# Denominators' columns moved onto the values' product, and two groups of products reordered, in a delta-rule attention kernel with an expert layer

## The chip, the cores and the metric

The kernel runs on one core of a Trainium2 chip. The metric is the device time of one execution in microseconds, as the median of several runs. One more execution was recorded by the hardware profiler; all rows below come from it. The engines are TensorE (PE, with its weight loads as PEld), VectorE (DVE), ScalarE (ACT), GpSimd (POOL) and SyncE (SP), which here only issues DMAs.

## The reference

Two sequences of 2048 rows of 128 numbers go through a linear attention layer with the delta rule, a layer norm, a layer of eight experts with top-2 routing and a capacity of 640 slots per expert and batch entry, and another layer norm.

```python
q, k = (x @ Wq), (x @ Wk)                 # 4 heads of 128
v, g = (x @ Wv), (x @ Wg)                 # 4 heads of 32
beta = sigmoid(x @ Wb)                    # one number per row and head
k = k * rsqrt(sum(k * k) + 1e-12);  q = q * 128 ** -0.5
# per row t:  delta = (v_t - k_t^T S) * beta_t;  S = S + k_t delta^T;  o_t = q_t^T S
o = o * rsqrt(mean(o * o) + 1e-5) * norm_w * silu(g)
x = layernorm(x + o @ Wo)
x = layernorm(x + moe(x))                 # top 2 of 8 experts, capacity, silu(h1) * h3 @ w2
```

## The kernel before, in words

**Tiling.** The recurrence is worked in 16 chunks of 128 rows, both sequences side by side. Within a chunk and head the deltas come from a triangular system of 128x128, whose inverse is built in levels: 16x16 blocks are inverted by elementwise steps on GpSimd (the first chunk on VectorE), and TensorE joins them to blocks of 32 (`z_32`, `w_32`), 64 (`z_64`, `w_64`) and 128 (`z_128`, `w_128`), each level being two groups of small products on tiles of 32x32 or 64x64 of the array. The right-hand side needs beta, which enters as the denominator 1 + exp(-x Wb) on the diagonal.

**Steps.** All engines run one loop of steps, `for p in range(NP + LAST)`, written out by hand: step p of TensorE does `keys` of chunk p, `values` of chunk p-1, the queries and the 32 and 64 levels of chunk p-4, the 128 level, deltas, new state and outputs of chunk p-5, and the projection of p-6. The order of the `at(...)` lines is the order on the engine. An engine waits in this order; nothing overtakes.

**Products in two forms.** `products` (lines 648 to 655) multiplies a weight matrix by the two sequences' 256 columns. For chunks 0 to 4 it is one float32 product. From chunk 5 (`XF`) on, both operands are split into a high and a low part of type float32r, and three one-pass products take its place. The split weights lie in tiles that the experts use later, so they are named `w13h` and `w13l` in the rows, and the split inputs `xeTh` and `xeTl`. `hb` is where the key-key products go.

**`values`** (line 669) makes, for each sequence, a float32 product with the inputs as the weights and the 128 columns of Wv streaming (line 672), which leaves rows on the partitions. Then `products` with the 4 columns of Wb as the weights makes the logits of beta, 4 partitions by 256 columns. ScalarE's `values_out` (line 1011) takes the exponential into `eb` and copies the values.

**The denominators' way.** SyncE stores `eb` to DRAM (`send_blocks`, line 520) and loads it back as 64 partitions by 16 (`load_blocks`, line 532), the form in which the 16x16 blocks are scaled; the blocks of the key-key product go the same way (`ab`), and so does their diagonal (`ssd`), which ScalarE's `key_norms` reads. SyncE does not send the blocks of a chunk before the loads of the chunk before have landed.

**Banks.** All products that ScalarE or VectorE carry off go through three PSUM banks in turn. A group in `STEP_FILLS` waits until the group three places before it has been carried off: `values` waits for the first of the two copies of `keys`, `key_key` for the second (and needs both for its operand).

**ScalarE's order** around the change is: norms of the heads (`head_norms`, line 1095, which waits for TensorE's `head_sums`), the two key copies, the copies of the diagonal blocks of 32, `values_out`, the high part of the inputs, and then at the head of the next step the copy of `z_128` and that of `key_key`.

The lines of TensorE's products by name:

| name | line | tile of the array |
|---|---|---|
| `products`, float32 / one-pass | 650 / 653 to 655 | full |
| `values` | 672 | full |
| `key_key`, `key_query` | 679, 694 | full |
| `z_32`, `w_32`, `z_64`, `w_64` | 708, 718, 728, 738 | 32x32 |
| `z_128`, `w_128` | 750, 762 | 64x64 |
| `state_keys` | 776 | 128x32 |
| `turn_keys`, `project` | 783, 852 | full |
| `head_sums` | 837 | full |

## Time and profile before

| what | value |
|---|---|
| median of 3 runs | 535.98 us (535.22 to 536.87) |
| the profiled execution | 539.49 us, span of its instructions 537.7 us |
| mean granted clock of TensorE | 0.961 |
| busy time TensorE | 490.4 us (91%), weight loads 408.4 us (76%) |
| busy time VectorE, ScalarE, GpSimd | 330.7, 332.4, 319.7 us (61%, 62%, 59%) |
| chain that ended last, by engine | TensorE 71%, DMA 9%, GpSimd 7% |
| DMA queue of SyncE and its like (q1) | 114864 packets, 29.60 MB, 27.0% of 16 engines |

The span divides into a start with round trips through DRAM (to about 82 us), steady attention steps (to about 254 us), the last attention steps, in which no new chunk begins, and from about 330 us on the experts and the last layer norm. The time of a product in a timeline includes its way through the array, so products that follow each other overlap there. The chain of waits counts each only from the end of the one before.

### The profile page before, as it was taken

What the parts mean: (1) busy time and instruction counts of PE and PEld (TensorE: products, weight loads), DVE (VectorE), ACT (ScalarE), POOL (GpSimd) and SP (SyncE); (2) the same over time, 40 slices, a digit from 0 to 9 for tenths busy, and PEclk for the clock granted to TensorE, in tenths of its full rate; (3) what the DMA queues carried; (4) which work ended last, traced back from release to release, by engine and by line L of the source; (5) the groups of instructions that cost most, each with busy time, mean ns of one, the idle gap of its engine ahead of it and who ended that gap; (6) DMA issues with size and microseconds to landing.
All of it is one profiled execution on the core that took longest, in us unless ns stands there. A gap on an engine that the chain in (4) does not pass through costs nothing.

```text
span 537.7 us, 18954 instructions
## 1 busy us (share of the span) xinstructions
PE 490.4 (91%) x7096; PEld 408.4 (76%) x7096; DVE 330.7 (61%) x1316; ACT 332.4 (62%) x916; POOL 319.7 (59%) x441
## 2 busy tenths in 40 slices
PE   6989999999999999999979977999999999999900
PEld 4666767767777777776656667999999999999900
DVE  4436567767687676876955872565455654555344
ACT  3646777777777877777743642554555545555456
POOL 3053528757578575785883452376677766767650
PEclk9999999999999999999985998999999999999975
DMA  3358753762545725436383234254555545553366
GB/s 93 31 86 226 257 112 44 107 93 31 66 46 59 102 33 72 49 46 99 34 166 39 27 33 109 36 109 55 108 107 76 109 55 108 93 85 36 31 135 204
DMA packets 136820, 45.83 MB, mean 85 GB/s; under 512 B 89568, under 2 KB 131296, under 8 KB 136736
## 3 DMA queue, kind: packets, MB, share of 16 engines
q1 hardware_dynamic: 114864, 29.60, 27.0%
q0 software_dynamic: 20288, 9.51, 19.4%
q10 hardware_dynamic: 1584, 5.59, 2.6%
q8 instruction: 54, 0.88, 0.7%
q14 instruction: 30, 0.25, 0.1%
HBM read 21.13 MB, written 23.55 MB: 83 GB/s over the span
## 4 chain that ended last, share of the span: by engine, by line
PE 71%; DMA 9%; POOL 7%; issue 5%; SPq 3%; ACT 2%; DVE 1%; POOLq 1%; ACTq 0%; DVEq 0%
PE ps L956 19%; PE ps L970 13%; PE ps L694 4%; PE ps L679 4%; POOL slots_in L1665 3%; PE ps L650 3%; PE ps L653 3%; PE ps L654 2%; PE ps L655 2%; POOL xs L1648 2%; PE ps L914 2%; PE ps L718 2%; POOL prod L1647 2%; DMA a_diag<-hb 1%; PE ps L728 1%
## 5 line engine op out<-in xcount | busy, mean ns | idle before, releaser
L1706 POOL DMA_INDIRECT x_store<-xk,row x80 | 123.9, 1549 | 68.5 <-ACT xk L1214 45.8
L1665 POOL DMA_INDIRECT slots_in<-x,slot x64 | 98.7, 1542 | 25.6 <-issue 17.3
L1540 DVE TENSOR_TENSOR hb<-ps,hs 128x320 f32<-128x320 f32 (+1 forms) x128 | 62.7, 491 | 53.1 <-ACT hs L1206 52.6
L1206 ACT ACTIVATE hs<-ps 128x320 f32<-128x320 f32 (+1 forms) x128 | 55.7, 435 | 34.5 <-PE ps L956 33.5
L970 PE MATMUL ps<-w2s,hb 128*128 128x128 f32 x640 | 74.1, 275 | 0.0
L970 PEld LDWEIGHTS ps<-w2s,hb 128*128 128x128 f32 x640 | 72.8, 192 | 0.0
L956 PE MATMUL ps<-xeTh,w13h 128*128 128x320 f32 x224 | 71.3, 318 | 0.9 <-DVE xeTl L1564 0.9
L956 PE MATMUL ps<-xeTl,w13h 128*128 128x320 f32 x224 | 69.9, 312 | 0.0
L956 PE MATMUL ps<-xeTh,w13l 128*128 128x320 f32 x224 | 69.9, 312 | 0.0
L1214 ACT ACTIVATE xk<-ps,gs 128x128 f32<-128x128 f32 x80 | 24.1, 364 | 45.4 <-PE ps L970 45.4
L1647 POOL TENSOR_TENSOR prod<-a,xs 128x28 f32<-128x28 f32 (+11 forms) x120 | 32.5, 271 | 25.5 <-DVE xs L1375 16.7
L956 PEld LDWEIGHTS ps<-xeTh,w13h 128*128 128x128 f32 x224 | 42.8, 191 | 1.1 <-issue 1.1
L1679 POOL TENSOR_TENSOR Vk<-V,sq 128x256 f32<-128x256 f32 x16 | 10.0, 627 | 56.4 <-ACT sq L1046 56.4
L956 PEld LDWEIGHTS ps<-xeTl,w13h 128*128 128x128 f32 x224 | 42.8, 191 | 0.0
L956 PEld LDWEIGHTS ps<-xeTh,w13l 128*128 128x128 f32 x224 | 42.8, 191 | 0.0
L1648 POOL TENSOR_TENSOR xs<-xs,prod 128x28 f32<-128x28 f32 (+11 forms) x120 | 33.9, 283 | 9.4
L1063 ACT ACTIVATE TT<-x32T 32x256 f32<-32x256 f32 x64 | 26.5, 414 | 18.0 <-DVE x L1318 17.5
L653 PE MATMUL ps<-xeTh,w13h 128*128 128x256 f32 (+1 forms) x110 | 36.2, 329 | 0.0
L694 PE MATMUL ps<-gq,xTs 128*128 128x512 f32 x64 | 34.5, 623 | 0.3 <-issue 0.3
L679 PE MATMUL ps<-y,xTs 128*128 128x512 f32 x64 | 34.0, 620 | 0.5 <-ACT eg L1034 0.5
L654 PE MATMUL ps<-xeTl,w13h 128*128 128x256 f32 (+1 forms) x110 | 31.0, 282 | 0.0
L655 PE MATMUL ps<-xeTh,w13l 128*128 128x256 f32 (+1 forms) x110 | 30.8, 280 | 0.0
(210 smaller groups left out, 1085.3 us busy)
## 6 DMA issues: line engine op xcount, KB each, us to landing
slots_in<-zeros ACTq DMA_DIRECT2D x10, 520.0 KB, 5.0
xe<-slots_in SPq DMA_DIRECT2D x15, 325.0 KB, 2.9
w<-w_in SPq DMA_DIRECT2D x8, 448.0 KB, 4.0
xTs<-xT SPq DMA_DIRECT2D x4, 512.0 KB, 5.1
a_diag<-hb SPq DMA_DIRECT2D x64, 32.0 KB, 1.9
inv<-xs SPq DMA_DIRECT2D x16, 128.0 KB, 2.7
xi<-inv SPq DMA_DIRECT2D x16, 128.0 KB
xk<-x SPq DMA_DIRECT2D x8, 256.0 KB, 4.0
```

Of the source, the lines that this page charges most:

```text
L653: mm(to, hi, xhs[:, r], start=True, stop=False)
L654: mm(to, hi, xls[:, r], start=False, stop=False)
L679: mm(ps[:, to, :], xTs[:, b, cols(n)], y[:, n % YR, b].rearrange("p h t -> p (h t)"), start=True, stop=True).then_inc(fill_mm, 1)
L694: mm(ps[:, to, :], xTs[:, b, cols(n)], gq[:, n % 2, b].rearrange("p h t -> p (h t)"), start=True, stop=True).then_inc(fill_mm, 1)
L956: last = mm(ps[:, HB[fill % 5], 0:HALF], w_[:, P * c:P * c + P], x_[:, par, cols], start=(t == 0), stop=(t == 2))
L970: last = mm(result_at(i), hb[:, par, c, P * i:P * i + P], w2s[:, we, c, :], start=(c == 0), stop=(c == FC))
L1206: af(hs[to, s % 4, :], ps[src, HB[fill_of(s) % 5], 0:HALF], ACT.Silu).then_inc(hs_ready, 1)
L1540: v.tensor_tensor(hb[rows_, par, c, HALF * g:HALF * g + HALF], ps[rows_, at, 0:HALF], hs[rows_, s % 4, :], ALU.mult).then_inc(h_ready, 1)
L1647: link(g.tensor_tensor(pr_, bc(a16[r, j + 1:, j], 2, j + 1), bc(xs[r, 0, j, 0:j + 1], 1, m), ALU.mult))
L1648: link(g.tensor_tensor(xs[r, 0, j + 1:, 0:j + 1], xs[r, 0, j + 1:, 0:j + 1], pr_, ALU.subtract))
L1665: g.indirect_dma_start(out=xs_d[:, :], out_offset=bass.IndirectOffsetOnAxis(ap=to, axis=0), in_=x1[:, p % 2, j, k, :], in_offset=None, com ...
L1706: g.indirect_dma_start(out=x1_d[:, :], in_=ye[:, par, i, :], in_offset=None, out_offset=bass.IndirectOffsetOnAxis(ap=row[:, par, i:i + 1], ...
```

## The change

The four columns of Wb stream behind the 128 columns of Wv, so that one product per sequence gives 132 columns. The exponentials then lie as 128 partitions by 2x4. They are stored to DRAM row by row (128 rows of 8 numbers) and loaded back one number at a time, and the semaphore for that load becomes two, one for even and one for odd chunks. The split of Wb into high and low parts goes. On TensorE `key_key` of the first sequence moves ahead of `z_128`, and `state_keys` ahead of `head_sums`; on ScalarE the copy of `key_key` moves ahead of that of `z_128`.

```diff
-    bd_d = nc.dram_tensor("den_store", (2, U, P), F32, kind="Internal").ap()
+    bd_d = nc.dram_tensor("den_store", (2, P, U), F32, kind="Internal").ap()
...
-        eb = sb("eb", [H, 2, 2 * P])
+        eb = sb("eb", [P, 2, B, H])
...
-                wait(sp, den_ld, 16 * (n - 1))
-                sp.dma_start(bd_d[n % 2].rearrange("(b h) t -> h b t", b=B),
-                             eb[:, n % 2].rearrange("h (b t) -> h b t", b=B)).then_inc(den_st, 16)
+                wait(sp, den_ld[n % 2], 16 * (n // 2))
+                sp.dma_start(bd_d[n % 2], eb[:, n % 2].rearrange("p b h -> p (b h)")).then_inc(den_st, 16)
...
-                sp.dma_start(denb[half], bd_d[n % 2].rearrange("u (k r) -> (u k) r", r=16)).then_inc(den_ld, 16)
+                sp.dma_start(denb[half].unsqueeze(2), bd_d[n % 2].rearrange("(k r) u -> u k r", r=16).unsqueeze(3),
+                             allow_slow_non_contiguous=True).then_inc(den_ld[n % 2], 16)
...
                 for b in range(B):
-                    mm(ps[:, to, P * b:P * b + P], xTs[:, b, cols(n)], wvb[:, 0:H * DV], start=True, stop=True)
-                products(ps[0:H, to, 256:512].rearrange("p (b t) -> p b t", b=B), wvb[:, H * DV:VW], wbs,
-                         n).then_inc(fill_mm, 1)
+                    last = mm(ps[:, to, VW * b:VW * b + VW], xTs[:, b, cols(n)], wvb[:], start=True, stop=True)
+                last.then_inc(fill_mm, 1)
...
                 at(turn_keys, p - 5)
+                at(key_key, p - 1, 0)
                 at(z_128, p - 5)
-                at(key_key, p - 1, 0)
...
+                at(state_keys, p - 4)
                 at(head_sums, p - 5)
-                at(state_keys, p - 4)
...
-                af(eb[:, n % 2], ps[0:H, src, 256:512], ACT.Exp, scale=-1.0).then_inc(den_out, 1)
+                both = ps[:, src, 0:B * VW].rearrange("p (b c) -> p b c", b=B)
+                af(eb[:, n % 2], both[:, :, H * DV:VW], ACT.Exp, scale=-1.0).then_inc(den_out, 1)
                 wait(act, vk_out, n - VR + 1)
-                af(V[:, n % VR], ps[:, src, 0:256].rearrange("p (b c) -> p b c", b=B), ACT.Copy).then_inc(v_out, 1)
+                af(V[:, n % VR], both[:, :, 0:H * DV], ACT.Copy).then_inc(v_out, 1)
...
+                at(key_key_out, p - 3, 0)
                 at(z128_copy, p - 7)
-                at(key_key_out, p - 3, 0)
...
-                dve.wait_ge(den_ld, 16 * n + 16)
+                for m in chunks_in(q):
+                    dve.wait_ge(den_ld[m % 2], 16 * (m // 2) + 16)
```

**TensorE, the middle of step 6,** from `z_64` to the keys' first product. Before:

```order
L728 MATMUL ps<-x32T,hb 32x32 x16
L837 MATMUL ps<-osq,heads 128x256
L776 MATMUL ps<-y,Zs 32x128 x8
L653 MATMUL ps<-xeTh,w13h 128x256
L654 MATMUL ps<-xeTl,w13h 128x256
```

After, where every line number is one or two lower:

```order
L726 MATMUL ps<-x32T,hb 32x32 x16
L774 MATMUL ps<-y,Zs 32x128 x8
L835 MATMUL ps<-osq,heads 128x256
L652 MATMUL ps<-xeTh,w13h 128x256
L653 MATMUL ps<-xeTl,w13h 128x256
```

`state_keys` (776, now 774) now stands directly behind `z_64`, one small-tile group behind another, so that `head_sums` (837, now 835) is followed by full products.

**TensorE, from `w_64` over the start of step 7 to `w_128`.** Before:

```order
L738 MATMUL ps<-z64,x32 32x32 x16
L672 MATMUL ps<-wvb,xTs 128x128 x2
L653 MATMUL ps<-xeTh,w13h 4x256
L654 MATMUL ps<-xeTl,w13h 4x256
L655 MATMUL ps<-xeTh,w13l 4x256
L783 MATMUL ps<-ident,KSt 128x128 x2
L750 MATMUL ps<-TT,hb 64x64 x8
L679 MATMUL ps<-y,xTs 128x512
L852 MATMUL ps<-wox,og 128x136 x2
L694 MATMUL ps<-gq,xTs 128x512
L762 MATMUL ps<-z128,x64 64x64 x8
```

After:

```order
L736 MATMUL ps<-z64,x32 32x32 x16
L671 MATMUL ps<-wvb,xTs 128x132 x2
L781 MATMUL ps<-ident,KSt 128x128 x2
L677 MATMUL ps<-y,xTs 128x512
L748 MATMUL ps<-TT,hb 64x64 x8
L850 MATMUL ps<-wox,og 128x136 x2
L692 MATMUL ps<-gq,xTs 128x512
L760 MATMUL ps<-z128,x64 64x64 x8
```

The three products with 4 columns of weights are gone, and `key_key` (679, now 677) and `z_128` (750, now 748) have changed places.

**ScalarE, the end of a step and the start of the next,** from the copies of the 32 blocks to those behind `w_128`. Before:

```order
L1072 ACTIVATE x64<-x32 32x4x32 x4
L1014 ACTIVATE eb<-ps 4x256
L1016 ACTIVATE V<-ps 128x256
L1135 ACTIVATE xeTh<-xTs 128x256
L1079 ACTIVATE z128<-ps 128x256
L1021 ACTIVATE hb<-ps 128x512
L1084 ACTIVATE TT<-ps 64x4x64 x2
```

After:

```order
L1071 ACTIVATE x64<-x32 32x4x32 x4
L1013 ACTIVATE eb<-ps 128x8
L1015 ACTIVATE V<-ps 128x256
L1134 ACTIVATE xeTh<-xTs 128x256
L1020 ACTIVATE hb<-ps 128x512
L1078 ACTIVATE z128<-ps 128x256
L1083 ACTIVATE TT<-ps 64x4x64 x2
```

The exponential has 8 columns for 256 on 128 partitions for 4, and the copy of `z_128` (1079, now 1078) stands behind that of `key_key`.

## Rows read from the trace of the kernel before

**Rows 1.** Windows: microseconds, then each engine's busy time, clock, DMA.

```profile
82.00:254.00 172.00, 171.52 (x3478) 125.92 (x3475) 126.95 (x554) 131.10 (x379) 120.92 (x216) 1.00 0.50 65
...
276.00:330.00 54.00, 44.74 (x764) 34.47 (x764) 33.19 (x150) 23.30 (x73) 26.86 (x21) 0.84 0.40 69
```

**Rows 2.** Chain of waits before 82 us: start, duration, what.

```profile
11.29 0.53 PE ps L650 x2
...
33.79 5.30 DMA xTs<-xT
...
45.65 0.52 PE ps L650 x2
...
64.42 5.38 DMA inv<-xs
...
73.13 0.14 issue
...
73.27 0.72 PE ps L708 x52
```

**Rows 3.** Chain of waits in a step: what each TensorE group takes.

```profile
78.78 0.63 PE ps L837 x2
...
79.41 0.57 PE ps L776 x16
...
79.98 0.32 PE ps L653
...
81.51 0.64 PE ps L672 x4
...
82.16 0.12 PE ps L653
```

**Rows 4.** Timeline of ScalarE: start, duration, line, what, count, idle before.

```profile
166.33 0.47 ACT L1098 ACTIVATE oln<-ps,eps 128x256 f32<-128x256 f32 x1 [0.24 <-PE ps L837]
...
167.16 1.25 ACT L1008 ACTIVATE y<-ps 128x512 f32<-128x512 f32 x2
...
169.58 0.37 ACT L1014 ACTIVATE eb<-ps 4x256 f32<-4x256 f32 x1
...
170.57 0.36 ACT L1079 ACTIVATE z<-ps 128x256 f32<-128x256 f32 x1
...
173.26 0.77 ACT L1084 ACTIVATE TT<-ps 64x256 f32<-64x256 f32 x2 [1.35 <-PE ps L762]
```

**Rows 5.** Timeline of TensorE, two steps' `values` among it.

```profile
151.10 0.71 PE L672 MATMUL ps<-wvb,xTs 128*128 128x128 f32 x4
...
165.60 0.70 PE L837 MATMUL ps<-osq,heads 128*128 128x256 f32 x2
...
168.33 0.71 PE L672 MATMUL ps<-wvb,xTs 128*128 128x128 f32 x4
...
172.53 0.68 PE L762 MATMUL ps<-z,x 64*64 64x64 f32 x16
```

**Rows 6.** Issues of two loads by tile: nanoseconds min/median/max, first and last start.

```profile
L537 SPq DMA_DIRECT2D denb<-den_store x16: 464/492/1421, 16.2 to 250.1; - x16
...
L541 SPq DMA_DIRECT2D ssd<-a_diag x16: 660/670/1845, 18.1 to 251.9; - x16
```

**Rows 7.** Windows around the first blocks' and diagonal's loads.

```profile
19.00:20.00 1.00, 1.00 (x4) 0.52 (x3) 0.00 (x0) 0.58 (x2) 0.00 (x0) 1.00 0.95 62
20.00:21.00 1.00, 1.00 (x5) 0.69 (x4) 0.61 (x3) 0.74 (x2) 0.00 (x0) 1.00 0.29 6
```

**Rows 8.** Waits, whole trace: VectorE for the denominators' load.

```profile
DVE denp L1365 <- DMA denb<-den_store: 2.2, 1, 2.2
```

**Rows 9.** Timeline of GpSimd, late in the attention part.

```profile
249.10 0.61 POOL L1679 TENSOR_TENSOR Vk<-V,sq 128x256 f32<-128x256 f32 x1 [4.35 <-ACT sq L1046]
```

**Rows 10.** Timeline of VectorE and TensorE at the entry of the inverse.

```profile
175.89 0.28 DVE L1302 TENSOR_SCALAR xh<-xi,high 128x128 f32<-128x128 f32 x1
...
177.44 0.73 PE L708 MATMUL ps<-xh,hb 32*32 32x16 f32 x64
```

More of the change, by code:

```diff
@@ L312, in build @@
         wgs = [w_[:, 2 * H * D:2 * H * D + H * DV] for w_ in wide]
-        wbs = [w_[:, 2 * H * D + H * DV:2 * H * D + H * DV + H] for w_ in wide]
         xhs, xls = (x_[:].rearrange("p a c -> p (a c)").rearrange("p (r b t) -> p r b t", r=XR, b=B)
@@ L367, in build @@
         den_st = sem("den_st")
-        den_ld = sem("den_ld")
+        den_ld = [sem("den_ld0"), sem("den_ld1")]
         a_st = sem("a_st")
@@ L1138, in weights_high @@
                 af(Mks[0], Mk[:], ACT.Copy)
-                af(wbs[0], wvb[:, H * DV:VW], ACT.Copy)
                 af(wgs[0], wg[:], ACT.Copy)
@@ L1489, in weights_low @@
                 dve.wait_ge(split_act, 1)
-                for parts, whole in ((Mks, Mk[:]), (wbs, wvb[:, H * DV:VW]), (wgs, wg[:]), (Nqs, Nq[:])):
+                for parts, whole in ((Mks, Mk[:]), (wgs, wg[:]), (Nqs, Nq[:])):
                     last = v.tensor_tensor(parts[1], whole, parts[0].bitcast(F32), ALU.subtract)
```

## The prediction

> **What bounds the kernel now.** I read the stretches by engine first, then the chain of waits, then single steps of the timeline. The stretches [rows 1] divide the attention part: from 82 to 254 us TensorE is busy for 171.52 of 172.00 us at a granted clock of 1.00, so every piece of TensorE work that goes away there can shorten the time. After 276 us the clock falls to 0.84 and TensorE waits often, and what bounds the stretch between is in the last point of the steady step. The expert part behind it contains nothing that the change touches.
>
> The chain of waits says what the time before 82 us hangs on [rows 2]. The first product of denominators lies on it (0.53 us at 11.29), then a series of round trips through DRAM in SyncE's queue (the last of them the input load of 5.30 us at 33.79, for which TensorE waits), then TensorE again with another such product (0.52 us at 45.65), then again DMAs (the load at 64.42 takes 5.38 us) until `z_32` starts at 73.27. From there the chain runs on TensorE alone.
>
> In a steady step I read the chain by ends, since the durations of the timeline overlap. It gives what each group really takes from the step [rows 3]. A full product after a group on small tiles is dearer than one after another full product: the keys' first takes 0.32 us after `state_keys`, where a one-pass product of 256 columns behind a full one takes 0.12. So a return from small tiles to full ones costs 0.20 us. `head_sums` (0.63) holds one such return, and `values` (0.64) another.
>
> **The change part by part, for one steady step.**
> 1. Three one-pass products of 4 columns go: 3 x 0.12 = 0.36 us [rows 3]. The values' two products get 132 columns for 128: 0.64 less the return of 0.20 is 0.44 us of streaming, and 4/128 of that is 0.014. Saving 0.35 us. This holds for chunks 5 to 15, which are 11 steps. Chunks 0 to 4 lose a two-instruction product of 0.52 us each instead [rows 2].
> 2. `state_keys` ahead of `head_sums`: the order 32x32, full, 128x32, full becomes 32x32, 128x32, full, full. `head_sums` keeps its return (0.63), the keys' first product behind it falls from 0.32 to 0.12. Saving 0.20 us, in the ten steps that have `head_sums` and keys after 73.27 us. `state_keys` itself is taken at its 0.57 us from either side; a spread of 0 to 0.2 is left for it.
> 3. `key_key` ahead of `z_128`: one return to full tiles is moved from `key_key` to `project`, none goes. Nothing is gained by streaming. `z_128` has its operands earlier than it needs them in either order.
>
> The sum of these would be 0.55 us per step. But edit 2 makes `head_sums` end later, and ScalarE's queue stands behind it: its logarithm, the exponential, then both copies of the keys. The next `values` needs the bank that the first of these copies empties (three fills back), and `key_key`, now second, needs both copies. In the timeline [rows 4, 5] `head_sums` ends at 166.30 (165.60 + 0.70), so `z_64` before it ended at 165.67 (less 0.63). ScalarE's logarithm starts at 166.33, and the first copy of the pair, which starts at 167.16 and takes half of the 1.25, ends at 167.78; `values` starts at 168.33, 0.55 us later. After the change `head_sums` ends at 165.67 + 0.57 + 0.63 = 166.87, 0.57 later, so that copy ends at 168.35. TensorE, by the sums above, would reach `values` at 168.33 - 0.20 = 168.13. It waits 0.22 us and then the way of the semaphore (up to 0.14 us, the gap in front of `z_32` at 73.27 [rows 2]); I take 0.27 in all. Waiting does not hide the return: I take `values` at its full 0.64 + 0.01 behind it. So of the 0.20 of edit 2 nothing is left and 0.07 is lost: 0.35 - 0.07 = 0.28 us per step. The second copy then ends at 168.98 (0.57 after today's 168.41) and `key_key` would start at about 169.2: no wait.
>
> Next in ScalarE's queue: today the copy of `z_128` starts at 170.57 and `w_128` at 172.53 [rows 4, 5], 1.6 us after that copy ended. Now that copy stands behind the one of `key_key` (0.50 more), and behind a queue that is 0.56 later, less about 0.1 for the exponential on 128x8 where 4x256 took 0.37. It ends near 172.0, and `w_128` would start at 172.2. The cover shrinks from 1.6 to about 0.2 us; if it is gone, each 0.1 missing costs 1 us over ten steps.
>
> VectorE runs on from the end of `w_64`, and only follows. The other loop, through GpSimd's solver and the DMA that brings the inverse back, has its result (`xh`) at 176.17 while `z_32` starts at 177.44 [rows 10]: 1.1 us of cover behind the semaphore, of which a faster TensorE eats 0.3 to 0.4. Behind 249.10 us GpSimd sets the pace, but its `Vk` there waited 4.35 us for ScalarE [rows 9], which follows TensorE: that point moves forward by all that the steps before it gained, and the rest keeps its length.
>
> Steady part: 10 steps (chunks 6 to 15, behind 73.27 us) x 0.28 = 2.8 us. From both sides: 0.20 per step if the wait costs 0.15 instead of 0.07 (2.0 us), and 0.55 if there is no wait (5.5 us). I take 2.8, since the copy's end and the reach of TensorE are each read from rows.
>
> **The DMA side.** The store of denominators becomes 128 pieces of 32 bytes for 8 of 512, the load back 1024 pieces of 4 bytes for 64 of 64. The nearest row for that load is the diagonal's, also 1024 elements of 4 bytes: SyncE issues it in 0.67 us (median) where the present load takes 0.49 [rows 6]. The blocks' and the diagonal's loads together, 2048 pieces, hold the 16 DMA engines at 0.95 of the microsecond from 19 to 20 and 0.29 of the next [rows 7], so 1024 pieces are 0.6 us of all engines. In a steady step both are covered: VectorE reads the load a step later, and in the whole trace it waited for it once, for 2.2 us, in the first chunk [rows 8], where it then waits for the blocks anyway. Before 73 us they are not always. The load's issue stands on the path once, ahead of the input load at 33.79 (+0.2), and its 0.6 us stand in a busy queue ahead of that load and ahead of the one at 64.42: 0 to 0.6 each, I take 0.3 each. Against that stand the two products that lie on the chain there, 0.53 and 0.52, less 0.01 each: 1.0 us. Net of the start: 1.0 - 0.2 - 0.6 = 0.2 us gained (bounds: 1.0 gained; 0.4 lost with both collisions whole).
>
> The Trainium skill, "DMA: Bandwidth & Descriptors", Rules for kernel authors, says that a non-contiguous last dimension lowers to one descriptor per element and advises against it. The diagonal's row agrees on the price of issuing (0.67 against 0.49 us). By that rule the load is worse for every chunk; by the rows it matters twice. If it counted in all 16 chunks at 0.6 + 0.2 us, it would take 12.8 us and the kernel would be slower; the single wait in rows 8 speaks against that. Its weaker form is rival D.
>
> **Sum.** 2.8 + 0.2 = 3.0 us. The profiled execution took 539.49 us (span 537.7) and would take 536.5; the median of the runs is 535.98, which gives 533.0.
>
> **Rivals.**
> A. The forecast, `values` waits a little on the keys' copy: 533.0. Chance 0.45.
> B. No wait shows, the whole 0.55 per step comes: 5.5 + 0.2 gives 530.3. For it: the two times that I compare (168.13 and 168.34) lie only 0.2 us apart, and ends on TensorE are modelled. Against it: ScalarE has no gap between the logarithm and the copies. Chance 0.22.
> C. ScalarE becomes the bound: `w_128` waits for the copy of `z_128` as well, 0.15 to 0.25 us per step. Then 0.05 to 0.13 is left per step, about 1 us in all: 535.0. For it: the cover of 0.2 us is thin. Against it: ScalarE had 1.35 us free in front of the copies behind `w_128` [rows 4], so it starts each step afresh. Chance 0.22, with all other ways in which the gain and a loss at the start cancel.
> D. Slower: the element-wise load delays the round trips of the start. There SyncE waits for the previous chunk's diagonal before it sends the next blocks, five rounds before 73 us. If the 1024 small pieces made each round 1.3 us longer (the diagonal's issue went up to 1.85 us once, 1.2 over its median [rows 6]), it would cost 6.5 us against the 1.0 and 2.8 gained: 537.7. The break-even is 0.8 us per round. Against it: the first of these loads is issued at 16.2 us [rows 6], and the engines are busy with the other two only from about 19 us on [rows 7]. Chance 0.11.
>
> **How the numbers follow.** A change of this kernel under 0.3% (1.6 us) can't be told from none. A and B are faster, except for A's low end (0.2 per step and a loss at the start, 1.6 us), which I give 0.03; C is mostly the same, with 0.04 of it faster; D is slower with 0.08 and the same with 0.03. That makes faster 0.68, the same 0.24, slower 0.08. The range runs from B's 530.3, widened by 0.2 for the spread of `state_keys`, to just past C, 536.2, which leaves out most of D.
>
> **What would show it.** In the profile after: the one-pass 128x4 products gone and the keys' first product behind `head_sums` at 0.12 in the chain (edits 1 and 2); idle time of TensorE in front of `values`, released by ScalarE's key copy, of 0.2 to 0.3 us in each steady step (A), none (B), or in front of `w_128`, released by the copy of `z_128` (C). A steady step, 17.22 us from one `values` to the next (168.33 less 151.10 by its start a step before), should be 16.94 under A, 16.67 under B, over 17.1 under C. `z_32` of step 6, now at 73.27, should stand between 72.3 and 73.7; at 75 or later D would hold. The forecast is wrong if the step is shorter and the end isn't, or if the low clock behind 276 us lasts a different time: at half clock, 1 us more of it costs 0.5.

## The result and the profile after

The changed kernel takes 533.38 us (median of 20 runs, 528.75 to 536.90), the kernel before 537.64 us beside it (20 runs, 533.32 to 541.34). The ratio is 0.9906 with a 95% interval of 0.9887 to 0.9926: faster by 4.3 us by the medians. The forecast was 533.0 us with a range of 530.1 to 536.2. That the two times lie 0.4 us apart is partly luck: the forecast took 3.0 us off a median of 535.98 us (3 runs of the kernel before), and over 20 runs that kernel has 537.64. In two later groups of runs, each on a chip of its own (called the second and the third chip below), the same kernel had ratios of 0.9943 [0.9913, 0.9973] and 0.9954 [0.9919, 0.9988], which is 3.1 and 2.5 us. The kernel before against itself, in the first group below, gave 0.9986 [0.9957, 1.0016].

The profiled execution took 533.38 us with a span of 531.6 (before: 539.49 and 537.7). Its page answers to the one of before so (busy time of the engines, clock and packets of DMA):

```profile
PE 482.6 (91%) x7053; PEld 404.9 (76%) x7053; DVE 330.5 (62%) x1315; ACT 328.6 (62%) x915; POOL 320.8 (60%) x441
...
PEclk9998999999999999999988997999999999999955
DMA packets 154164, 45.83 MB, mean 86 GB/s; under 512 B 107040, under 2 KB 148640, under 8 KB 154080
```

The clock of the kernel before was:

```profile
PEclk9999999999999999999985998999999999999975
```

The digit 8 in the fourth slice of the clock, at 40 us, is new; more of it below. The two stretches of [rows 1] now read:

```profile
82.00:254.00 172.00, 169.45 (x3501) 124.98 (x3496) 129.63 (x564) 131.07 (x385) 124.27 (x217) 1.00 0.54 66
276.00:330.00 54.00, 46.68 (x742) 37.96 (x742) 35.70 (x157) 25.87 (x76) 25.98 (x20) 0.88 0.42 79
```

In the same 172 us the trace has 23 more matmuls, and TensorE is idle for 2.55 us instead of 0.48; 1.6 of these are ten waits of 0.16 us in front of `values`, one per step. The chain of waits through one step (start, duration, what; against [rows 3]) shows the wait and the new order:

```profile
149.01 0.57 PE ps L774 x16
149.58 0.64 PE ps L835 x2
...
150.25 0.48 ACT oln L1097
...
151.08 0.59 ACT y L1006
...
151.71 0.72 PE ps L671 x4
...
152.65 0.86 PE ps L677 x2
153.51 0.61 PE ps L748 x16
154.12 0.66 PE ps L850 x4
```

`state_keys` (L774) keeps its 0.57 us ahead of `head_sums` (L835, 0.64), and the chain then leaves TensorE for ScalarE's logarithm and its first copy of the keys before it comes back at `values` (L671). The return to full tiles stands at `project` (L850, 0.66 us) and no longer at `key_key` (L677, 0.86), as the third point of the prediction had it. The timelines of TensorE and ScalarE in the same step, against [rows 4, 5]:

```profile
151.71 0.72 PE L671 MATMUL ps<-wvb,xTs 128*128 128x132 f32 x4 [0.16 <-ACT y L1006]
...
155.57 0.68 PE L760 MATMUL ps<-z,x 64*64 64x64 f32 x16
...
168.63 0.60 PE L671 MATMUL ps<-wvb,xTs 128*128 128x132 f32 x3 [0.16 <-ACT y L1006]
```

```profile
153.31 0.18 ACT L1013 ACTIVATE eb<-ps 128x8 f32<-128x8 f32 x1
...
154.72 0.38 ACT L1078 ACTIVATE z<-ps 128x256 f32<-128x256 f32 x1
```

A step is 168.63 - 151.71 = 16.92 us, for 17.22 before. The exponential on 128x8 takes 0.18 us for 0.37, and the copy of `z_128` ends at 155.10, 0.47 us ahead of `w_128`. Over the whole trace (total, times, longest) the wait in front of `values` and VectorE's wait of [rows 8] are:

```profile
PE ps L671 <- ACT y L1006: 1.8, 11, 0.2
DVE denp L1364 <- DMA denb<-den_store: 3.5, 1, 3.5
```

At the other two marks, the start of `z_32` in step 6 ([rows 2], 73.27) and GpSimd's `Vk` ([rows 9], 249.10), the chain of waits and the timeline give:

```profile
74.40 0.72 PE ps L706 x52
```

```profile
247.90 0.61 POOL L1678 TENSOR_TENSOR Vk<-V,sq 128x256 f32<-128x256 f32 x1 [3.70 <-ACT sq L1045]
```

So the start lost 1.13 us, and at 248 us the kernel is 1.20 us ahead: the steps between have given 2.33. The other 4.9 of the 6.1 us between the two spans came later. Windows of ten microseconds behind 276, of the kernel before and then of the changed one (the number before the last two is the granted clock), show where:

```profile
276.00:286.00 10.00, 7.44 (x168) 4.97 (x170) 5.17 (x20) 4.77 (x15) 7.65 (x7) 0.57 0.97 197
286.00:296.00 10.00, 9.62 (x122) 6.54 (x119) 6.78 (x32) 3.03 (x9) 1.79 (x2) 0.58 0.18 16
```

```profile
276.00:286.00 10.00, 9.37 (x195) 6.30 (x196) 7.11 (x22) 5.60 (x17) 7.22 (x7) 0.68 0.88 186
286.00:296.00 10.00, 10.00 (x243) 7.72 (x242) 8.37 (x45) 6.58 (x22) 2.06 (x3) 1.00 0.20 30
```

The kernel before ran at 1.2 GHz for nearly all of both windows, the changed one for most of the first alone. Whether that belongs to the change is what the second profiles of both kernels answer, below.

### The profile page after: what moved, and what is told of

The parts are those of the page before. It is cut to its first block, busy times and chain, and to the rows that moved or that the text cites. A ratio compares the mean times of both kernels' runs of the same rounds, so it can differ in the third digit from the quotient of the medians.

```text
span 531.6 us, 18873 instructions
## 1 busy us (share of the span) xinstructions
PE 482.6 (91%) x7053; PEld 404.9 (76%) x7053; DVE 330.5 (62%) x1315; ACT 328.6 (62%) x915; POOL 320.8 (60%) x441
## 4 chain that ended last, share of the span: by engine, by line
PE 69%; DMA 8%; POOL 7%; issue 5%; ACT 4%; DVE 3%; SPq 2%; POOLq 1%; ACTq 0%; DVEq 0%
PE ps L954 19%; PE ps L968 13%; PE ps L692 4%; PE ps L677 4%; POOL slots_in L1664 3%; PE ps L649 3%; PE ps L652 2%; POOL xs L1647 2%; PE ps L912 2%; PE ps L716 2%; POOL prod L1646 2%; PE ps L844 2%; PE ps L671 2%; PE ps L706 1%; PE ps L818 1%
## 5 line engine op out<-in xcount | busy, mean ns | idle before, releaser
L1646 POOL TENSOR_TENSOR prod<-a,xs 128x28 f32<-128x28 f32 (+11 forms) x120 | 33.8, 281 | 26.7 <-DVE xs L1374 17.9
L677 PE MATMUL ps<-y,xTs 128*128 128x512 f32 x64 | 33.4, 612 | 1.2 <-ACT y L1006 0.7
L652 PE MATMUL ps<-xeTh,w13h 128*128 128x256 f32 x99 | 33.1, 335 | 0.0
L653 PE MATMUL ps<-xeTl,w13h 128*128 128x256 f32 x99 | 27.9, 281 | 0.0
L654 PE MATMUL ps<-xeTh,w13l 128*128 128x256 f32 x99 | 27.8, 281 | 0.0
```

The costliest lines, as they stand in the source:

```text
L652: mm(to, hi, xhs[:, r], start=True, stop=False)
L653: mm(to, hi, xls[:, r], start=False, stop=False)
L677: mm(ps[:, to, :], xTs[:, b, cols(n)], y[:, n % YR, b].rearrange("p h t -> p (h t)"), start=True, stop=True).then_inc(fill_mm, 1)
L1646: link(g.tensor_tensor(pr_, bc(a16[r, j + 1:, j], 2, j + 1), bc(xs[r, 0, j, 0:j + 1], 1, m), ALU.mult))
```

## The experiments

Twelve more kernels ran (three of them repeat the two above), four at a time on one chip, each timed against the kernel before on that chip. The first four shared a median of 538.40 us for it, the next four (second chip) 542.53, the last four (third chip) 542.31. Only ratios, and times of one group, are compared. "Step" is the distance from one start of `values` to the next, from 115 us on (the two before it have another length in every kernel), and "start" is the start of `z_32` in step 6.

### The two kernels once more

The kernel before, unchanged. 

> The kernel before, unchanged, profiled a second time. Theory (the change saves 0.30 us per steady step and gives 1.1 us back before 73 us; what is left of the difference between the two profiles, 5.3 us between z_32 of step 19 and of step 20, is the length of a low clock that differs from execution to execution): the steady step is 17.22 us again and z_32 of step 6 lies near 73.3, but the time from 276 us on may differ by some us from the first profile, with the low clock. Rival (the low clock is shorter because of the change): the half clock lasts some 18 us again, from about 276 to 294, and step 19 to 20 takes 22.2 us again. Ratio 1.000 within 0.2% either way.

The changed kernel, on the second chip and on the third. 

> The changed kernel, unchanged, profiled a second time. Theory: step 16.92 us, z_32 of step 6 near 74.4, again 0.16 us of wait in front of values; the length of the low clock behind 275 us may be another than the first profile's 6 us. Rival (the change shortens the low clock): about 6 us again. Ratio to before 0.991.

> The changed kernel once more, as the standard for the three beside it and as a second look at its start. A steady step (one start of values to the next) is 16.92 us by every account. If the drop of TensorE's clock at 38 to 45 us hangs on the idle time in front of the products of the input load (0.93 and 1.06 us in the first profile of it), it comes again wherever these two gaps are near 1 us, and z_32 of step 6 starts at 74 or later; without the drop it starts near 72.

| | ratio, interval | step | start | clock low behind 276 us |
|---|---|---|---|---|
| before, first profile | | 17.22 | 73.27 | 17 us |
| before again | 0.9986 [0.9957, 1.0016] | 17.23 | 72.21 | 7 us |
| changed, first profile | 0.9906 [0.9887, 0.9926] | 16.92 | 74.40 | 6 us |
| changed, second chip | 0.9943 [0.9913, 0.9973] | 16.92 to 18.00 | 71.62 | none |
| changed, third chip | 0.9954 [0.9919, 0.9988] | 16.93 to 17.86 | 72.30 | 3 us |

The last column is worked out from windows between 276 and 296 us: twice the share of the clock that is missing, times their length (20 x 0.43 + 20 x 0.42 for the first). So the same program has the low clock there for 17 us in one execution and for 7 in another (windows of the second profile of the kernel before, then of the changed kernel on the second chip):

```profile
276.00:286.00 10.00, 5.73 (x156) 3.77 (x156) 5.08 (x19) 4.76 (x15) 7.07 (x7) 0.67 0.93 192
286.00:296.00 10.00, 9.20 (x178) 7.12 (x180) 8.71 (x39) 5.10 (x15) 2.05 (x2) 0.99 0.18 16
```

```profile
276.00:286.00 10.00, 5.97 (x204) 4.30 (x204) 6.46 (x22) 4.76 (x15) 6.46 (x6) 1.00 0.96 195
286.00:296.00 10.00, 9.17 (x208) 7.26 (x207) 8.22 (x41) 6.79 (x22) 2.65 (x2) 1.00 0.27 36
```

Ten microseconds more or less at half clock are 5 us of time, as much as the 4.9 us by which the first two profiles differ behind 248 us. So that part of their difference can't be put down to the change. The 20 runs of the changed kernel say the same: the four fastest (528.75 to 530.28 us) have a mean granted clock of 0.970 to 0.976, the other sixteen (531.72 to 536.90) one of 0.957 to 0.967. Of the clock the Trainium skill ("TensorE: Matmul & The Clock Gate", What's actually happening) says that the chip judges TensorE's activity by a beat that runs free of the kernel, and that the point at which it acts varies for that reason. The two profiles of one program do vary, but by 10 us, where that page gives the variation as half a microsecond; that the beat makes it is not shown here.

On the second and third chip single steps are up to 1 us longer than their neighbours; the others are called undisturbed here. From 80 us on, nine steps take 155.78 and 155.85 us in the two profiles of the kernel before and 153.68 in the first of the changed one, but 156.52 and 157.78 on the second and third chip, where the kernel before was not profiled. So the ratios of 3.1 and 2.5 us there agree with the forecast, but the profiles there don't show that the gain comes from the steps. What the long steps wait for is taken up behind the experiments.

### The columns alone

The changed kernel with the other two edits taken back:

```
-                at(key_key, p - 1, 0)
                 at(z_128, p - 5)
+                at(key_key, p - 1, 0)
...
-                at(key_key_out, p - 3, 0)
                 at(z128_copy, p - 7)
+                at(key_key_out, p - 3, 0)
...
-                at(state_keys, p - 4)
                 at(head_sums, p - 5)
+                at(state_keys, p - 4)
```

> Only the four columns on the values' product with their new way through DRAM; both reorderings undone. Theory (the columns give 0.35 per step, state_keys ahead of head_sums gives nothing because the time it frees is waited for on the keys' copy): steady step 17.22 - 0.35 = 16.87 us, no wait of values on ScalarE's key copy, z_32 of step 6 about 1.1 us later than before. Rival (the order of the groups matters for the gain): step 17.0 or more. Against the time before: 2 to 3.5 us faster in the median.

Measured: 534.79 us, 0.9923 [0.9882, 0.9964]; but the step is 17.09 to 17.12 us (the last 17.19), a gain of 0.13 where 0.35 were expected, and the start is at 75.28. The chain of waits shows what took the rest:

```profile
152.60 0.65 PE ps L671 x4
...
153.47 0.14 issue
153.61 0.68 PE ps L748 x16
```

`z_128` (L748) now stands right behind `values` and the turned keys, 0.36 us earlier than before, TensorE waits 0.14 us at it, and its group is 0.68 long for 0.61. That gives back 0.21 of the 0.35. The chain names no releaser, but one of its operands is VectorE's copy of the level of 64:

```profile
152.66 0.85 DVE L1332 TENSOR_SCALAR TT<-ps 32x256 f32<-32x256 f32 x2 [0.68 <-PE ps L736]
```

It ends at 153.51, 0.10 us before `z_128` starts. In the kernel before it ends at 152.10, and `z_128` starts at 152.31 in the timeline, 0.21 us later and without a wait. In the changed kernel `key_key` runs at that place for 0.86 us, and `z_128` follows at its plain 0.61.

### The state's keys alone, and the changed kernel without them

Edit 2 on the kernel before (`state_keys` ahead of `head_sums`), and the changed kernel with that edit taken back (the same lines the other way round):

```
+                at(state_keys, p - 4)
                 at(head_sums, p - 5)
-                at(state_keys, p - 4)
```

> Only state_keys ahead of head_sums, on the kernel before. Theory: the keys' first product falls from 0.32 to about 0.12, values waits 0.16 to 0.3 us on the key copy, the step is 17.22 + 0.05 = 17.27 us, and the time is the same or 0.5 us slower. Rival (no wait in this form, since the three 4-column products lie behind): step 17.02, 2 us faster.

Measured: 537.39 us, 0.9956 [0.9925, 0.9986], and a step of 17.27, 0.05 longer than before. The wait is there as forecast. The chain leaves `head_sums` (L837) at 151.05, passes ScalarE's logarithm and its first copy, and enters `values` (L672):

```profile
150.41 0.64 PE ps L837 x2
...
151.07 0.48 ACT oln L1098
...
151.90 0.59 ACT y L1008
...
152.53 0.71 PE ps L672 x4
```

> The changed kernel with head_sums ahead of state_keys again. Theory (the move of state_keys gives 0.20 on TensorE and costs 0.25 through the wait): the wait in front of values is gone, the keys' first product takes 0.32 again, the step is 16.87 us, 0.05 less than the changed kernel's 16.92, and the time is 0.5 us less or the same. Rival (the wait was short of the gain): step over 16.95.

Measured: 540.45 us, 0.9973 [0.9940, 1.0007]. The undisturbed steps of its trace (three of seven) are 16.91 to 16.95 us, the same as with the edit, and nothing waits in front of `values`. By the steps edit 2 is worth 0.00 within the change; the times (540.45 beside 538.28, intervals that overlap) don't tell the two apart.

### The keys' first product alone

Edit 3 on the kernel before, TensorE's and ScalarE's order both:

```
+                at(key_key, p - 1, 0)
                 at(z_128, p - 5)
-                at(key_key, p - 1, 0)
...
+                at(key_key_out, p - 3, 0)
                 at(z128_copy, p - 7)
-                at(key_key_out, p - 3, 0)
```

> Only key_key ahead of z_128 with the copies in the same order on ScalarE, on the kernel before. Theory: one return to full tiles moves from key_key to project, the step stays at 17.22 us and the time the same within 0.1%. Rival (z_128 waited for VectorE's copy of the 64 level before and key_key now covers that): step 17.0 to 17.1, 1 to 2 us faster.

Measured: 537.34 us, 0.9965 [0.9939, 0.9991], a step of 17.22 to 17.23 (the last 17.27). Alone it gives nothing. The times of this kernel and of the one with edit 2 alone lie 1 us under the median of before without a shorter step; their intervals end just under 1 (0.9986 and 0.9991) but overlap with that of the kernel before against itself, so they measure how far a time can be trusted here.

### Both copies of the keys ahead of the logarithm

The changed kernel, ScalarE's queue alone:

```
-                at(head_norms, p - 7)
...
                 at(keys_out, p - 2, 0)
+                at(head_norms, p - 7)
```

> The changed kernel with ScalarE's first key copy ahead of the norms of the heads, so that it no longer stands behind head_sums. Theory (values waits for that copy and nothing else): no wait in front of values, the step falls from 16.92 to 16.67 us, and over ten steps 2.5 us are gained on the changed kernel. Rival (the second key copy, the z_128 copy or the norms, now half a microsecond later, take the wait's place): a wait in front of key_key, project or w_128, step between 16.75 and 16.92.

Measured: 538.11 us, 0.9945 [0.9909, 0.9980], beside 0.9943 of the changed kernel on that chip. The wait in front of `values` is gone and the undisturbed step is 16.69 us (16.67 had been worked out for no wait):

```profile
170.59 0.72 PE L671 MATMUL ps<-wvb,xTs 128*128 128x132 f32 x4
...
187.28 0.72 PE L671 MATMUL ps<-wvb,xTs 128*128 128x132 f32 x4
```

But only two of the seven steps are like that. Others wait at the next places of the same queue, as this line, of the step before, shows:

```profile
154.57 1.12 PE L677 MATMUL ps<-y,xTs 128*128 128x512 f32 x2 [0.50 <-ACT y L1006]
```

The nine steps from 80 us on take 155.89 us together there, and 156.52 in the changed kernel's profile on the same chip. A gain of 0.6 us is too small to show in the time.

### One more load of the denominators in the kernel before

The kernel before, with a second, element-wise load of the denominators into a tile of its own behind the first (its result is not used):

```
                 sp.dma_start(denb[half], bd_d[n % 2].rearrange("u (k r) -> (u k) r", r=16)).then_inc(den_ld, 16)
+                wait(sp, den_x, 16 * (n - 1))
+                sp.dma_start(denx[half].unsqueeze(2), bd_d[n % 2].rearrange("u t -> (u t)").rearrange("(r p) -> p r", r=16).unsqueeze(2),
+                             allow_slow_non_contiguous=True).then_inc(den_x, 16)
```

> The kernel before plus one load per chunk of 1024 single elements from the denominators' store into a tile that nothing reads, issued right behind the denominators' load. It measures the element-wise load by itself, here on top of the old one. Theory (SyncE's issue of the next load becomes 0.4 to 0.9 us longer behind an element-wise one, and this counts only before 73 us): the blocks' load takes 1.0 us to issue (0.59 before), z_32 of step 6 comes 1.5 to 2.5 us later, the steady step stays 17.22 us, 1.5 to 2.5 us slower in all. Rival (it costs in every step too): step 17.3 or more, over 3 us slower. Rival (the start of the changed kernel was late for another reason): z_32 of step 6 within 0.3 us of 73.3.

Measured: 546.39 us, 1.0077 [1.0037, 1.0117], 4.2 us by the ratio. The start is at 75.05 where two profiles of the kernel before have 73.27 and 72.21: 1.8 to 2.8 us later. Five of these loads are issued before it, so one more load costs 0.4 to 0.6 us a round where SyncE's round trips are the chain; rival D had 1.3. That is about what SyncE takes to issue the added load (0.60 us, median). The blocks' load behind it was expected to take 1.0 us to issue, and takes 0.67:

```profile
L545 SPq DMA_DIRECT2D ab<-a_diag x16: 573/671/1960, 18.4 to 259.2; - x16
```

A second load of the old form was not run, so how much of the cost is due to the single elements is not shown. The steps are 17.63 to 18.24 us; how much of that is the load's and how much this chip's stays open, since the kernel before was not profiled there.

### More idle products in step 4

In four of the traces above with the columns on the values' product, the low clock comes at 38 to 45 us. The kernel keeps TensorE busy there with 22 idle products; this one has 26, and 5 more behind `z_32`:

```
                 if p == 4:
-                    keep_on(22)
+                    keep_on(26)
                 at(z_32, p - 4)
+                if p == 4:
+                    keep_on(5)
```

> The changed kernel with more of the idle products of step 4: 26 for 22 in front of z_32, and 5 more behind it, in the two gaps of about 1 us that TensorE has there (nothing of the result hangs on them). The theory, that the gaps left by the three columns' products drop the clock at 38 to 45 us: no slice under full clock there, z_32 of step 6 between 71.5 and 73.0 instead of 74.4, and 1 to 2 us off the time wherever the changed kernel has the drop. The rival, that the start is late because of SyncE's queue (the element-wise load): the clock is full there and z_32 stays at 74 or later, same time. The extra products cost nothing by either, unless they end behind the operands of z_32: 4 x 0.23 = 0.92 us for a gap of 0.93.

Measured: 542.28 us, 1.0019 [0.9987, 1.0052], where the changed kernel beside it has 539.23. The gaps are filled, the clock is full and the start is at 71.79, in its range. Yet the median is 3 us longer (the two intervals, [0.9987, 1.0052] and [0.9919, 0.9988], just touch), which neither theory had. In the profile, two engines stall at once in a steady step (VectorE, then ScalarE; in brackets the idle time before and its releaser):

```profile
184.56 0.85 DVE L1325 COPY z<-ps 32x256 f32<-32x256 f32 x2 [2.15 <-remote]
```

```profile
185.42 0.47 ACT L1099 ACTIVATE oln<-ps,eps 128x256 f32<-128x256 f32 x1 [2.70 <-remote]
```

TensorE is idle for 1.48 of the 4 us around them, and its clock falls:

```profile
184.00:188.00 4.00, 2.52 (x43) 2.14 (x42) 3.02 (x10) 2.53 (x7) 3.39 (x3) 0.90 1.15 117
188.00:192.00 4.00, 4.00 (x26) 2.01 (x24) 3.23 (x16) 2.18 (x7) 0.82 (x4) 0.67 0.24 21
```

That step and the next are 18.81 and 18.53 us. "Remote" is what the view calls another core or an unknown queue. The DMA engines are full in that window (1.15).

### The load issued last

The changed kernel, with the element-wise load behind those of the blocks and of the diagonal:

```
-                sp.wait_ge(den_st, 16 * n + 16)
-                sp.dma_start(denb[half].unsqueeze(2), ...
...
                 sp.dma_start(ssd[:, n % 3, :].unsqueeze(2), diagonal, ...
+                sp.wait_ge(den_st, 16 * n + 16)
+                sp.dma_start(denb[half].unsqueeze(2), ...
```

> The changed kernel with the element-wise load of the denominators issued behind the two loads of the blocks and of the diagonal, instead of ahead of them. SyncE's queue as the cause of the late start: the blocks' load is issued in about 0.6 us again instead of 1.0 and a round trip is 0.6 to 1.0 us shorter, so z_32 of step 6 comes 1 to 3 us earlier. The rival, that the round trip ends with the load that lands last, whichever it is (VectorE needs blocks and denominators for the same instruction): z_32 within 0.3 us of the changed kernel's when both have the same clock at 40 us, and the same time. The steady step is 16.92 by both.

Measured: 543.18 us, 1.0030 [0.9991, 1.0069], 4.0 us behind the changed kernel beside it. Both theories fail. The blocks' load is issued in 0.61 us again (median; 1.31 in step 4), but VectorE now waits 6.1 us for the denominators in the first chunk. In the changed kernel it waits 3.5 us for them and then 1.1 for the blocks, 4.6 in all:

```profile
DVE denp L1364 <- DMA denb<-den_store: 6.1, 1, 6.1
```

In step 4 `z_32` waits 2.38 us for VectorE's `xh`, the clock drops (0.61 from 38 to 46 us), and the start is at 78.18:

```profile
39.31 0.83 PE L706 MATMUL ps<-xh,hb 32*32 32x16 f32 x64 [2.38 <-DVE xh L1300]
```

So with this load issued last, VectorE has all its operands later than with it issued first. That the issue time of the other two is what it lands in is a reading, and no run tests it.

### Copies first and more idle products

The two edits of the kernels above together. 

> The changed kernel with ScalarE's two copies of the keys ahead of its logarithm and exponential of the norms, and with the idle products of the kernel e7 (26 and 5). If the wait of 0.16 us in front of values is all that stands between edit 2 and its 0.20, a steady step is 16.70 instead of 16.92 and ten of them give 2.2 us; the start as in e7. The rival, that the queue of ScalarE hands the delay on (the reciprocal root of the norms comes 1.2 us later, and what hangs on it with it): steps between 16.7 and 17.4 by turns, as one profile on another chip showed, and no gain in the mean.

Measured: 539.04 us, 0.9956 [0.9926, 0.9986], beside 0.9954 of the changed kernel on that chip. Steps are 16.73 to 17.93 us by turns: the rival's picture. It has the same idle products as the kernel that was 3 us slower, so these alone are not what made that one slow. No version that ran is measurably faster than the changed kernel.

## Why the prediction was right, and where it was not

**The steady step.** Forecast A had a step of 16.94 and a wait of 0.2 to 0.3 us in front of `values`, released by ScalarE's key copy; measured are 16.92 us and a wait of 0.16, eleven times. The sum had 0.27 for the wait. Behind it `values` takes 0.72 us in the chain instead of 0.65 without a wait (in the kernel with the columns alone), so the two together cost 0.23. Against C, `w_128` did not wait: the copy of `z_128` ended 0.47 us ahead of it, for the 0.2 worked out. Against B, the step never was 16.67; it came to 16.69 only where the wait was taken away (in two of seven steps), 0.23 less than 16.92. So the wait is what edit 2's 0.20 turns into.

**The split among the edits was wrong in one sentence**: "`z_128` has its operands earlier than it needs them in either order." With the columns' products gone it has not: in the kernel with the columns alone, 0.21 of edit 1's 0.35 goes to `z_128`. Edit 3, priced at nothing, gives these back, though alone on the kernel before it gives nothing either. That holds for the order of before, with the three products still in front of it; once they are gone the group moves forward by 0.36 us, and that was not followed up. The sum came out right because the change has both edits.

| | worked out | measured |
|---|---|---|
| columns alone | -0.35 | -0.13 |
| `state_keys` alone | +0.07 | +0.05 |
| `key_key` alone | 0 | 0.00 |
| columns and `key_key` | -0.35 | -0.30 |
| all three | -0.28 | -0.30 |

With edit 2 the step is as long as without it, so the loss of 0.07 that was to be taken off the 0.35 is not there, and the 0.35 itself is 0.30. Where the missing 0.05 goes was not found.

**The number of steps.** Ten times 0.28 were counted. In the first profile the two first steps (17.89 and 17.31 us for 17.61 and 17.60) gave nothing and eight gave 0.30 each: 2.4 for 2.8.

**The start.** 0.2 us gained and `z_32` at 72.3 to 73.7 was the forecast; the first profile has 74.40, 1.13 later than before, outside it. Two things meet in step 4. The denominators' products of 0.52 us that go stand ahead of a place where TensorE soon idles: without them the idle products end at 36.96 instead of 37.38. And SyncE comes to the load of the inverse (`xi`) later. In the chain of waits, before and then after, the blocks' load (L539, L538) and that load (L517, L516) are:

```profile
31.71 0.60 SPq L539
...
33.06 0.69 SPq L517
```

```profile
31.93 1.50 SPq L538
...
34.19 0.58 SPq L516
```

From the start of the denominators' load there to that of `xi` it is 1.94 us in the four profiles with the old load alone, and 2.91 to 3.07 in the eight with the element-wise load issued first. VectorE's `xh`, which `z_32` needs, ends at 37.75 instead of 36.95. So TensorE waits 0.93 us in front of `z_32`, two thirds of it because of the queue, and 1.06 for the input load (1.09 before). Ahead of `z_32` there is no idle time in either profile of the kernel before.

```profile
37.90 0.72 PE L706 MATMUL ps<-xh,hb 32*32 32x16 f32 x64 [0.93 <-DVE xh L1300]
39.67 1.80 PE L649 MATMUL ps<-xTs,Mk 128*128 128x256 f32 x4 [1.06 <-DMA xTs<-xT]
```

```profile
38.00:46.00 8.00, 6.94 (x186) 4.56 (x184) 2.97 (x7) 2.25 (x5) 5.05 (x15) 0.79 0.65 125
```

The input's products start 0.54 us later than before (39.67 for 39.13). The clock in these eight microseconds is 0.79, and from those products to the next `values` it is 7.14 us, for 5.81 and 5.79 in the kernel before and 5.65 in the two other profiles of the changed one: the low clock costs 1.3 to 1.5 us. All profiles counted: of the five kernels with the products of before (the kernel before twice, edits 2 and 3 alone, the extra load), none has the low clock at 38 to 48 us. Of the seven profiles with the columns moved and the idle products as they were, five have it; the two with them lengthened have none. Where it stays away, the changed kernel starts at 71.62 and 72.30 us, for 73.27 and 72.21 before. The two of before lie 1.06 us apart, so a gain of 0.2 is neither shown nor refuted. Where it comes, the start is at 73.43 to 75.28 (78.18 with the load issued last). The sizes of the gaps alone don't decide: 0.62 and 1.28 us without a drop, 0.61 and 1.19 with one. The prediction counted the two products as 1.0 us gained without asking what the engine does with the time, had 0.5 us for the longer queue at this place where 0.97 are measured, and named the clock as a risk only behind 276 us. Whether the products that go or the slower queue matter more for the low clock was not tried apart.

**The DMA side.** SyncE's rows by tile (nanoseconds min/median/max, first and last start; the load of the denominators against [rows 6]), the blocks' load in the kernel before first:

```profile
L539 SPq DMA_DIRECT2D ab<-a_diag x16: 579/592/605, 17.5 to 251.3; - x16
...
L535 SPq DMA_DIRECT2D denb<-den_store x16: 611/626/716, 16.5 to 249.1; - x16
L538 SPq DMA_DIRECT2D ab<-a_diag x16: 593/991/1939, 17.6 to 250.2; - x16
```

The load's issue takes 0.63 us (0.67 was taken), but the load right behind it takes 0.99, for 0.59 in the kernel before (0.90 and 0.98 in the two other profiles of the changed kernel). This 0.4, 0.9 in step 4, was not in the sum, and at the start the chain passes through it. Why it is longer is not shown: behind the extra load of the experiment it took 0.67. The Trainium skill's rule that each element becomes a descriptor ("DMA: Bandwidth & Descriptors", Rules for kernel authors) agrees with the packets, 17344 more. That section gives no price for issuing them. That this would cost in all 16 chunks is refuted by steps of 16.92 us; its weaker form, rival D, is half true: the queue does get longer, by 0.97 us in step 4 and by 0.4 to 0.6 a round with the extra load, and not by 1.3. Rival D's own time was added up wrongly: 535.98 + 6.5 - 1.0 - 2.8 is 538.7, and not 537.7.

**The end.** `Vk` was to move forward "by all that the steps before it gained": it moved by 1.20, the 2.33 of the steps less the 1.13 of the start, where 3.0 were forecast. The second profiles show how far this mark can be trusted: it is at 249.10 and 248.12 us in the two of the kernel before, and at 247.90, 248.08 and 250.03 in the three of the changed one (the last two on other chips). So up to here no pair of profiles shows the 3.0 us. That the medians (4.3, 3.1 and 2.5 us by the ratios) lie around it is measured, but how the gain divides between the attention steps and what comes behind them is not shown, and the agreement with the sum is in part luck. Behind it the rest kept its length but for the low clock, whose length varies between executions of one program by up to 10 us at half clock. Whether the first ratio (0.9906) is better than the two others (0.9943, 0.9954) by that luck is not shown: the intervals overlap, and the clocks of the 20 runs of the kernel before beside the first ratio are not on record.

What stays open: why single steps are up to 1 us longer on the second and third chip, in kernels with and without each edit. In the changed kernel's profile on the third chip ScalarE's copy `dT` starts late three times, 1.4 us in all, with nothing shown but a product that had long ended; in that with more idle products two engines wait for "remote" at once, and the kernels without edit 2 (second chip) and with the load issued last have one such wait each, of 1.9 and 2.1 us. And why the kernel with more idle products alone is 3 us slower over twelve runs, when the same with the copies first is not.

## What to carry to other kernels

Before work is taken off a full engine, look at what stands right behind it: the group moves forward by the same amount, and its operands may not be ready. An edit that is worth nothing alone can be what lets another keep its gain, so price edits together, and undo them one by one as well as doing them one by one. Work that is removed ahead of a place where the engine waits anyway is no gain there, and a longer wait can bring the low clock. A load that replaces another in a queue is priced with what stands behind it in the queue, and not by its own issue alone.

When a ratio is off the sum by less than a per cent, compare marks inside the profiles (a start, a step, an entry of the next stage) and take a second profile of both kernels before the difference is explained.

## What the runs showed of the hardware

- One program has TensorE at 1.2 GHz for 17 us in one execution and for 7 in the next at the same place (276 us), and another for 6, 3 and 0; the four fastest of the changed kernel's 20 runs (up to 530.28 us) have a mean clock of 0.970 to 0.976, the others 0.957 to 0.967.
- An element-wise load of 1024 pieces of 4 bytes is issued by SyncE in 0.63 us where the one of 64 pieces of 64 bytes took 0.49, and in the changed kernel the load issued right behind it takes 0.99 us instead of 0.59 (1.50 in step 4, in every profile with this order); behind an extra load of 1024 single elements on top of the old one it took 0.67.
- A group on tiles of 128x32 takes 0.57 us in the chain both behind a full product (kernel before) and behind tiles of 32x32 (changed); the return to full tiles costs 0.20 us, which the keys' first product paid before (0.32) and no longer pays (0.12: in the timeline it ends at 150.33, `head_sums` at 150.21).
- ScalarE's exponential takes 0.18 us on 128x8 for 0.37 on 4x256: both have 1024 elements, so here the length of the row counts, and not their number.
